# Decoder layer on one core: second head's weights staged apart, first value projection in other banks, mantissa steps spread, last down products by token tile

## What is computed

```python
q, k, v = (x @ (codes * repeat(scales, 32, axis=0)) + bias for each of q, k, v)   # 16 heads of 128
attn = softmax(q @ k.T / sqrt(128))
x = layernorm(x + (attn @ v) @ Wo + bo)                  # Wo from codes and scales as well
x = layernorm(x + cross_attention(x, ctx))               # 1024 context rows, the 54 largest scores of each row
x = layernorm(x + (silu(x @ Wg.T) * (x @ Wu.T)) @ Wd.T)  # 2048 inner features
```

## Time and profile before

| | before |
|---|---|
| median of 3 runs (lowest, highest) | 995.46 us (993.17, 996.73) |
| profiled execution: time, span | 997.53 us, 995.6 us |
| TensorE busy | 931.1 us, 94% |
| VectorE, ScalarE, GpSimd busy | 65%, 56%, 40% |
| mean granted TensorE clock | 0.984 |

### The profile page before, as it was taken

The page is one execution under the profiler, slowest core; times in us unless marked ns, Lnnn a source line. Parts: engine busy times, 40 slices in busy tenths (PEclk is TensorE's granted clock), DMA queues, the critical chain, the costliest instruction groups (busy, mean ns, idle before and its releaser), DMA issues.

```text
span 995.6 us, 13034 instructions
## 1 busy us (share of the span) xinstructions
PE 931.1 (94%) x4498; PEld 755.6 (76%) x4498; DVE 646.0 (65%) x1261; ACT 553.0 (56%) x1141; POOL 398.5 (40%) x315
## 2 busy tenths in 40 slices
PE   9899989998999989999998989979999899999996
PEld 7677767776778777777766878878878788788885
DVE  4668776878777787767786599894778314511114
ACT  4646665666755667666775556453473644443331
POOL 3337321241322315243533256651674662354440
PEclk9999999999999999999999999979999999999998
DMA  7332220021301113122211122430443251243321
GB/s 228 100 90 70 69 80 17 27 81 56 87 27 28 57 48 103 36 63 68 74 50 57 44 85 75 115 97 15 135 116 95 77 156 33 77 136 102 98 74 43
DMA packets 46099, 76.95 MB, mean 77 GB/s; under 512 B 5584, under 2 KB 11216, under 8 KB 45776
## 3 DMA queue, kind: packets, MB, share of 16 engines
q1 hardware_dynamic: 45600, 75.68, 26.1%
q10 hardware_dynamic: 432, 0.39, 0.1%
HBM read 73.69 MB, written 2.36 MB: 76 GB/s over the span
## 4 chain that ended last, share of the span: by engine, by line
PE 73%; DVE 20%; ACT 3%; DMA 1%; issue 1%; POOL 1%; SPq 1%; DVEq 0%; ACTq 0%; POOLq 0%
PE p L99 68%; DVE JK L441 4%; PE p L468 3%; DVE PT L478 3%; DVE QK L361 2%; DVE PR L459 2%; DVE acc L427 1%; DVE OT L498 1%; DVE st L530 1%; DVE WV L277 1%; DMA acc<-in_xT 1%; SPq L86 1%; PE p L721 1%; DVE m L668 1%; DMA SCL<-in_sq 1%
## 5 line engine op out<-in xcount | busy, mean ns | idle before, releaser
L441 DVE TENSOR_SCALAR_CACHE_REDUCE JK<-p,ssc 128x512 bf16<-128x512 f32 x112 | 83.7, 747 | 99.6 <-PE p L99 99.5
L99 PE MATMUL p<-R 128*128 128x512 f32 x544 | 138.5, 397 | 4.7 <-ACT V L384 3.8
L596 POOL TENSOR_TENSOR V<-RAW,V 128x512 fp32r<-128x512 f32 x64 | 82.8, 1314 | 144.1 <-ACT V L595 144.1
L449 ACT ACTIVATE PR<-p,nms,ssc 128x512 f32<-128x512 f32 x112 | 87.3, 780 | 78.8 <-DVE JK L441 78.4
L99 PE MATMUL p<-QK 128*128 128x512 f32 x384 | 118.8, 418 | 8.0 <-DVE QK L361 6.7
L99 PEld LDWEIGHTS p<-R 128*128 128x128 f32 x544 | 102.6, 190 | 30.2 <-ACT V L384 4.2
L99 PE MATMUL p<-R,V 128*128 128x512 f32 x480 | 112.8, 390 | 0.7 <-ACT C L595 0.7
L277 POOL TENSOR_TENSOR R<-RAW,R 128x512 fp32r<-128x512 f32 x38 | 51.2, 1350 | 153.9 <-ACT R L274 153.7
L273 POOL TENSOR_TENSOR RAW<-RAW,SCL 128x512 f32<-128x512 f32 x67 | 88.7, 1335 | 42.4 <-DMA SCL<-rq 17.0
L99 PEld LDWEIGHTS p<-R,V 128*128 128x128 f32 x480 | 89.9, 188 | 19.8 <-issue 1.1
L826 DVE TENSOR_TENSOR SX<-p,SX 128x512 f32<-128x512 f32 x32 | 22.1, 691 | 119.6 <-PE p L99 112.9
(11 more groups left out here) (151 smaller groups left out, 1623.4 us busy)
## 6 DMA issues: line engine op xcount, KB each, us to landing
RAW<-in_wg SPq DMA_DIRECT2D x32, 256.0 KB, 2.9
RAW<-in_wu SPq DMA_DIRECT2D x32, 256.0 KB, 2.7
RAW<-in_ctxn SPq DMA_DIRECT2D x32, 256.0 KB, 2.9
RAW<-in_wd SPq DMA_DIRECT2D x32, 256.0 KB, 2.8
RAW<-in_wq SPq DMA_DIRECT2D x20, 256.0 KB, 2.9
RAW<-in_wk SPq DMA_DIRECT2D x19, 256.0 KB, 2.7
RAW<-in_wv SPq DMA_DIRECT2D x16, 256.0 KB, 2.7
RAW<-in_wo SPq DMA_DIRECT2D x16, 256.0 KB, 3.6
```

Of the source, the lines that this page charges most:

```text
L99: return e.matmul(outp, a, b, start=st, stop=sp_)
L441: tm = op(dve, lambda e: e.tensor_scalar(JK[:, :], ps, nsc, None, ALU.mult, ALU.min, accum_out=m), T[("S", i)], T.get(("max", i - 1)), T.g ...
L449: T[("exp", i)] = op(act, lambda e: e.activation(PR[:, i % 3, :], ps, ACT.Exp, bias=m, scale=sc, accum_out=rs[:, i % 4:i % 4 + 1]), T[("ma ...
L596: tl = op(pool, lambda e: e.tensor_tensor(lo, raw, hi, ALU.subtract), th, free)
```

## The change

Four edits. (1) Codes and scales of head 1's weights are transferred at the very start into SX0 and BO, ahead of the last two pieces of the first value weights, and multiplied there (`own`). The first value projection goes to p2, p3, p4 and one of p5 to p7, and its evacuations stand ahead of the two checks. (2) The mantissa steps are a generator `factor()`; its small tiles lie in `st6`; it takes one to four steps at the end of each of the first quarters. Its loads wait for head 1's weights, since they reuse SX0. (3) `coefficients` moves from quarter 8 to 16, `add_bo` from steps j = 2 and 4 to 1 and 3, the load of BO to quarter 0. (4) The down products of the last three inner blocks are issued at the end, by token tile (`down_last`), and each tile is finished while the next one's products run; tiles 0 to 2 are normalized on ScalarE. The last block's split goes to CN2.

```diff
+        def piece_a(key, hi, lo, src, ssrc, sview, free, em, el, ready=None, pre=None, own=None):
+            k = npiece[0] % 4
+            if own is None:
+                npiece[0] += 1
...
+            raw = RAW[:, k, :] if own is None else own
...
-                v_first.extend([(-1, P[4][:, :])] + [fbank() for _ in range(3)])
+                v_first.extend([(k, P[5 + k][:, :]) for k in (-3, -2, -1)] + [fbank()])
...
+        def hh(n, x):
+            return CN2[:, 0, x, :] if n == 2 * NM - 1 else HH[:, n % 2, x, :]
...
+        def down_last():
+            act_table(ACT.Sqrt)
+            last = range(2 * NM - 3, 2 * NM)
+            def d(n, tt):
...
+            d(last[0], 0)
+            d(last[1], 0)
+            d(last[0], 1)
+            for tt in range(4):
+                for n in last[(2, 1, 0, 0)[tt]:]:
+                    t = d(n, tt)
+                r, ps = 4 + tt, P[tt][:, :]
+                row = acc[:, r]
+                if tt == 3:
+                    finish()
+                t = op(dve, lambda e, row=row, ps=ps: e.tensor_tensor(row, ps, row, ALU.add), t, T[("acc", r)])
+                if tt in (1, 2):
+                    finish()
+                t = op(dve, lambda e, r=r, row=row: e.bn_stats(st6[:, r, :], row), t)
+                ta = op(dve, lambda e, r=r: e.bn_aggr(mv[:, r, :], st6[:, r, :]), t)
+                ts = op(act, lambda e, r=r: e.activation(sd[:, r:r + 1], mv[:, r, 1:2], ACT.Sqrt, bias=eps_t[:, 0:1]),
+                        ta, t_eps)
+                def finish(tt=tt, r=r, row=row, ta=ta, ts=ts):
+                    t = op(dve, lambda e: e.reciprocal(rstd[:, r:r + 1], sd[:, r:r + 1]), ts)
+                    if tt < 3:
...
+                        t = op(act, lambda e: e.activation(row, row, ACT.Identity, bias=nm, scale=rstd[:, r:r + 1]), t)
+                    else:
+                        t = op(dve, lambda e: e.tensor_scalar(
+                            row, row, mv[:, r, 0:1], rstd[:, r:r + 1], ALU.subtract, ALU.mult), t)
+                    T[("out",)] = out_s.load(out[r], row, t)
+            finish()
...
+        def factor():
...
+                sc0_s.load(sr[:, w], ss.rearrange("a (b c) -> (a b) c", c=256), [W[("qk", 1, i)] for i in range(2)])
...
+        own1 = [SX0[:, w * 512:(w + 1) * 512] for w in range(2)]
+        pre1 = []
+        for w, src, ss in ((0, wq, sq), (1, wk, sk)):
+            scl = BO[:, w * 128:(w + 1) * 128]
+            pre1.append((one_s[2 * w].load(own1[w], src[1]), one_s[2 * w + 1].load(scl, bc8(ss, 1)), scl))
...
-        prep_qk(1, 0)
+        prep_qk(1, 0, pre=pre1[0], own=own1[0])
...
-        now[0] = 0
-        run_checks()
+        flush()
         for kt in range(1, 4):
             proj_v_first(kt)
         evacs()
-        flush()
+        T[("Tev", -2)], T[("Tev", -1)] = bank[2], bank[3]
+        now[0] = 0
+        run_checks()
...
+            if i == 0:
+                steps = factor()
+            if i < 11:
+                for _ in range((1, 2, 2, 2, 4, 0, 0, 1, 1, 1, 1)[i]):
+                    next(steps, None)
...
-            if i in (3, 4):
-                factor_a(t_s, i - 3)
-            if i == 5:
-                factor_b(t_s)
...
-            if i == 8:
+            if i == 16:
                 T_CF = coefficients()
-            if j in (2, 4):
-                add_bo(2 * (j - 2) + qt)
+            if j in (1, 3):
+                add_bo(2 * (j - 1) + qt)
...
-            down(n - 1)
-            load_wd(n + 2)
-            if n % NM == 0:
-                ffn_end(n // NM - 1)
+            if n < 2 * NM - 2:
+                down(n - 1)
+                load_wd(n + 2)
+            elif n == 2 * NM:
+                down_last()
+            if n == NM:
+                ffn_end(0)
```

More of the change, by code:

```diff
@@ L200, in decoder_layer @@
         bqk_s = Slot("s_bqk")
+        one_s = [Slot(f"s_one{i}") for i in range(4)]
         sc0_s = Slot("s_sc0")
@@ L821, in act_gu @@
             g, u = P[kg][:, :], P[ku][:, :]
-            hf, hi, lo = HF[:, s, :], HH[:, s, 0, :], HH[:, s, 1, :]
-            fr = [T.get(("down", n - 2)), T[("xsl", 1)]]
+            hf, hi, lo = HF[:, s, :], hh(n, 0), hh(n, 1)
+            fr = [T.get(("down", n - 2)), T[("xsl", 1)], T[("cnuse", 31)] if n == 2 * NM - 1 else None]
             t = op(act, lambda e: e.activation(hf, g, ACT.Silu), T[("g", n, 0)], T.get(("hl", n - 2)), T[("TX", 1)])
@@ L831, in down @@
         def down(n):
[L832 removed]
+            m = n % NM
             for tt in range(4):
                 c = slice(tt * 128, (tt + 1) * 128)
[L835 removed]
+                t = mm(P[tt][:, :], three(hh(n, 0)[:, c], hh(n, 1)[:, c], WD[:, n % 3, 0], WD[:, n % 3, 1]),
                        T[("hl", n)], T[("wd", n)], bank[tt] if m == 0 else None, start=m == 0, stop=m == NM - 1)
@@ L840, in decoder_layer @@
         out_s = Slot("s_out")
+        def down_last():
+            act_table(ACT.Sqrt)
+            last = range(2 * NM - 3, 2 * NM)
+            def d(n, tt):
+                c = slice(tt * 128, (tt + 1) * 128)
+                return mm(P[tt][:, :], three(hh(n, 0)[:, c], hh(n, 1)[:, c], WD[:, n % 3, 0], WD[:, n % 3, 1]),
+                          T[("hl", n)], T[("wd", n)], start=False, stop=n == 2 * NM - 1)
+            d(last[0], 0)
[18 more added lines that the diff above has]
+                    if tt < 3:
+                        nm = nms[:, tt:tt + 1]
+                        t = op(dve, lambda e: e.tensor_scalar(nm, mv[:, r, 0:1], rstd[:, r:r + 1], -1.0,
+                                                              ALU.mult, ALU.mult), t, ta)
+                        t = op(act, lambda e: e.activation(row, row, ACT.Identity, bias=nm, scale=rstd[:, r:r + 1]), t)
[4 more added lines that the diff above has]
+            finish()
         def ffn_end(b):
@@ L920, in decoder_layer @@
         t_sv0 = sv0_s.load(sv0, sv[:, 0:512].unsqueeze(1).to_broadcast((16, 8, 512)))
+        wv0 = [raw_s[2 + kt].load(RAW[:, 2 + kt, :], wv[0, kt]) for kt in range(2)]
+        own1 = [SX0[:, w * 512:(w + 1) * 512] for w in range(2)]
[3 more added lines that the diff above has]
+            pre1.append((one_s[2 * w].load(own1[w], src[1]), one_s[2 * w + 1].load(scl, bc8(ss, 1)), scl))
         prep_qk(0, 0, dve, dve, pre_q)
@@ L926, in decoder_layer @@
         flush()
-        wv0 = []
-        for kt in range(4):
-            k = (2 + kt) % 4
-            wv0.append(raw_s[k].load(RAW[:, k, :], wv[0, kt], raw_free[k]))
+        for kt in range(2, 4):
+            wv0.append(raw_s[kt - 2].load(RAW[:, kt - 2, :], wv[0, kt], raw_free[kt - 2]))
         misc_s.load(bv_t[:, :], bv)
```

55 lines of the change are left out of this document (28 added, 27 removed).

## The result

The changed kernel takes 982.78 us (median of 6 runs, 982.56 to 988.29), the kernel before 995.77 (6 runs): a ratio of 0.9883, interval 0.986 to 0.9906 (the two medians alone give 0.987; one of the six runs took 988.29). So 13.0 us are gone by the medians, 9.4 to 13.9 by the interval; the forecast was 11.8, to 983.7.

The account below looks back on a forecast made before the run. TensorE, busy 94%, bounds the kernel, so time comes only from its idle times, half-clock stretches and the end. 5.4 + 3.9 - 0.4 + 2.9 = 11.8 us gives 983.7; bounds 981.0 to 989.2, 8 in 10 for 980 to 988.5.

Parts of the forecast that it names:

- The start, 5.4: Ahead of head 1's first projection: 3.83 us idle and the slow clock behind it go; gain 5.4, between 3.6 and 5.5.
- it begins head 1's weights 5 us earlier than now: At the start: GpSimd, even 2 us after the value pieces, begins multiplying head 1's weights 5 us earlier.
- What is late next: After the start: VectorE, with splits of x and scaling queued, is 0.1 to 1.2 us late; 0.1 taken.
- the splits of x were the lower bound: Reading given to a gap of over 1 us ahead of quarter 2's value projection in the next profile.
- the last sign of a wrong prediction: In quarters 1 to 6: prediction wrong if TensorE waits for VectorE for more than 1 us.
- Mantissa steps, 3.9: Ahead of quarter 7's transposes: spreading steps removes the 2.30 us wait and slow clock; gain 3.9, between 1.7 and 4.0.
- Coefficients, -0.4: Moved from quarter 8 to 16: 0.8 won, 1.2 paid; net 0.4 lost, between 1.2 lost and 1.1 won.
- The end, 2.9: Last product to end: 9.1 us becomes 6.0, less 0.2 of waiting; gain 2.9, between 2.0 and 3.9.
- the prediction's third rival: The clock falls elsewhere: a slow stretch may come or go, 1.7 us either way, 982 or 985.4; 10%.
- VectorE stays the bound: Rival: in VectorE's full quarters stalls return in small pieces, each part at its lower bound, 6.3 us, 989.2; 15%.
- the value pieces come late: Rival: at the start, added transfers delay the last two value pieces, 5 us of waiting, 990; 5%.
- collisions (0.9 each): Rival: GpSimd and VectorE hinder each other, quarters 4 to 7; 0.92 each, 13 eat the gain, 16 give 999; 3%.

Follow-up runs that it names:

- x_early: Changed kernel with head 1's weights through shared buffers, old banks, checks ahead of evacuations and early mantissa loads, the bias load staying moved: 988.89 us, ratio 0.9937.
- x_flag: Changed kernel with all four checks of the first value weights ahead of the loop, so their sum reaches TensorE a quarter earlier: 986.12 us, ratio 0.9902.
- x_steps: Changed kernel with the mantissa steps in three bursts again, in quarters 3, 4 and 5: 985.46 us, ratio 0.9906.
- x_raw: Changed kernel with only the staging of head 1's weights undone (shared buffers again), new banks and order kept: 984.16 us, ratio 0.989.
- x_tail: Changed kernel with the old end: 12 down products behind the last block, four tiles finished one after the other: 985.84 us, ratio 0.9911.
- x_lastadd: Changed kernel with the fourth tile's addition ahead of the third tile's reciprocal and small product: 984.5 us, ratio 0.9888.
- x_onlybanks: Kernel before with only the four banks of the first values changed and the evacuations put ahead of the checks: 994.89 us, ratio 0.9997.
- x_start: Changed kernel with head 1's weights through shared buffers, old banks and checks ahead of evacuations, mantissa loads still late: 986.18 us, ratio 0.9912.
- x_coef26: Changed kernel with the coefficients in quarter 26 instead of 16: 983.77 us, ratio 0.9886.

## Why the prediction was right, and where it wasn't

**The start, 5.4.** Size right (9.59 to 4.28 behind the value products, 5.3), reason off, so that luck has a part in it. "Now ten are", of the transfers ahead of head 1's weights, holds; but what counts of it are the four mantissa loads that stood between, and then banks and order. The step "it begins head 1's weights 5 us earlier than now" is true and worth 0.4 only, beside the new banks. The steps add up to 4.6 (3.3 for banks and order, 0.9 for the four loads, 0.4 for the place of its own). The other 0.7 lies between x_early and the kernel before, where GpSimd starts at 21.71 and at 23.05 behind the same transfers; no run explains it.

**What is late next.** The sign to look for, a gap of over 1 us ahead of quarter 2's value projection, came (1.06) and was misread: "the splits of x were the lower bound" fell with x_flag. VectorE is late, by 0.4 where 0.1 was taken: quarter 2's row maximum begins at 31.43, its scores were done at 31.01. But a gap stood there before as well, 0.88, with VectorE idle ahead of that row maximum:

```profile
36.68 0.69 DVE L441 TENSOR_SCALAR_CACHE_REDUCE JK<-p 128x512 bf16<-128x512 f32 x1 [0.63 <-PE p L99]
...
41.52 2.09 PE L99 MATMUL p<-WV,R 128*128 128x512 f32 x8 [0.88 <-DVE JK L441]
```

So the splits can explain 0.2 of the 1.06 at the most, and the start gave its full 5.3. The trace puts the 1.06 down to VectorE; by the letter the last sign of a wrong prediction, over 1 us of waiting for VectorE in quarters 1 to 6, came with it. x_flag shows that the wait was for the flag.

**Mantissa steps, 3.9.** 4.2 from quarter 7 to 9, 4.0 undone by x_steps.

**Coefficients, -0.4.** The 1.2 lost in quarters 16 to 19 are right (1.15). Of the 0.8 to be won at 8 to 10, some 1.2 came at quarter 11 and 1.1 went at 13, where scaling and GpSimd collide; at 23 a gain of 0.8 stands where the earlier trace rows had such a collision. Together about -0.3 from quarter 9 to 114, near the -0.4 forecast, by terms that the prediction didn't have: that is luck.

**The end, 2.9.** 3.4 won behind the last product, 0.45 lost ahead of it (0.2 forecast): 2.95. The step "starts 0.5 to 0.6 us late" is the 0.52 measured.

**The rest.** These terms give 9.1 at quarter 114 and 12.0 at the end; the profiles differ by 13.7. From quarter 114 to 127 another 1.4 came from slow stretches: two stood at 516 and 533, one stands at 522. That is the prediction's third rival, on the lucky side. Of the others, "VectorE stays the bound" fell (the gap ahead of quarter 7 is gone), "the value pieces come late" too (no gap ahead of them), and of collisions (0.9 each) a few came, not 13: four scalings in the first 80 us took 0.89 to 1.40. Of the six long mantissa steps (two of them have one input only) one took 0.90, the others 0.41 to 0.48. The lower bounds of the terms add up to 6.1 us, not 6.3, twelve products take 2.88, not 2.7, and the earlier trace rows names the exponential for the 0.70, not the low half; none of this changes the forecast by more than 0.2.

**What stays open** is why the clock falls at one place and not at another. With the coefficients in quarter 16, nine of the profiles show the same three gaps between 99 and 109 us, 0.60, 0.77 and 0.77; behind them the clock fell in x_raw, x_tail, x_flag and x_lastadd (1.0 us each) and stayed at 1.00 in the other five. With the coefficients moved, which leaves two of them, it stayed in all three. A long idle time doesn't decide it either. Row and window of the changed kernel in the cross-attention:

```profile
772.90 1.33 PE L723 MATMUL p<-ident,SX 128*128 128x128 f32 x8 [2.64 <-DVE SX L681]
```
```profile
772.90:777.00 4.10, 4.05 (x21) 3.31 (x22) 0.14 (x1) 3.85 (x8) 4.10 (x4) 1.00 0.12 44
```

Here the clock stayed at 1.00; behind the same wait, of 2.62 to 2.67, it fell in the 13 other profiles. Not shown is whether any edit here changes the chance of a fall elsewhere, or only draws again.

## What to carry to other kernels

Find the gain by the lead at each repeated instruction, not by busy shares: the same list shows which term of a sum held, and where a collision or a slow stretch took it back. When an idle time goes, look for what TensorE waits for next within some 10 us: in x_onlybanks the next two waits and the slow clock beside them took back 3.9 of 4.8 us within a quarter. And when undoing a part gives less than its term, look for what came along with it; here four small loads and a held queue stood beside the staging that the change was named after, and with the new banks the staging was the least of it.

## What was not expected of the hardware

- The granted clock fell to 0.50 (1.2 of 2.4 GHz) behind idle times far shorter than the 2.30 and 3.83 us of before: behind 0.60, 0.77 and 0.77 us, and behind 0.55 and 1.11. After one of 1.92 alone (x_start) and one of 2.64 (the changed kernel, at 773) it stayed at 1.00.
- A slow stretch of 3.4 us cost 1.5 to 1.7 us where TensorE had work throughout (x_flag at 219, x_coef26 at 346, x_early at 30), and 1.0 at 104 us, in quarters where VectorE was late anyway.
- An edit that won 1 us at its place lost 3 in the median, with three more such stretches in its profile (x_flag); that the edit brought them is not shown.
